# Scores of the wide layers cut into 64-row tiles, with the special keys in columns of their own

## What is computed

```python
q, k, v = x @ Wq, ctx @ Wk, ctx @ Wv              # (2048,1024), (1601,1024) twice; 16 heads of 64
logits = einsum('hqd,hkd->hqk', q, k) / 8
logits[:, :, token_indices_A] -= 20 * (1 - mask_A)[:, None]   # two keys
logits[:, :, token_indices_B] -= 20 * (1 - mask_B)[:, None]   # two keys
x = x + softmax(logits) @ v @ Wo + bo
```

## Time and profile before

| | us |
|---|---|
| median of 3 runs | 4620.56 |
| lowest, highest | 4617.27, 4621.11 |
| the profiled execution | 4619.93 |
| span of its trace | 4618.1 |

### The profile page before, as it was taken

One profiled execution on the slowest core, in us unless ns is written; L12 is line 12 of the kernel. 1 busy time (PEld: TensorE's weight loads), 2 busy tenths in 40 slices (PEclk: granted clock), 3 DMA queues, 4 the chain that ended last, 5 costly groups with the idle time before them and its releaser, 6 DMA issues.

```text
span 4618.1 us, 56243 instructions
## 1 busy us (share of the span) xinstructions
PE 4523.6 (98%) x20489; PEld 2807.1 (61%) x20489; DVE 2989.6 (65%) x5016; ACT 2262.0 (49%) x4016; POOL 2674.4 (58%) x1281
## 2 busy tenths in 40 slices
PE   8999999999999979999999999999999999999999
PEld 7888865555556545555556555555556655565554
DVE  3321467667766678778746667766767667676766
ACT  3222454454445436666655444444455545454443
POOL 0000367797778611111036887788774877788775
PEclk9999999999999979999999999999999999999999
DMA  4555832221222021011233221222216212222220
GB/s 151 178 188 163 289 79 64 66 68 45 66 64 52 12 39 16 12 15 16 58 109 111 67 67 45 64 68 52 52 46 221 63 39 64 64 68 54 58 48 28
DMA packets 124629, 349.64 MB, mean 76 GB/s; under 512 B 28085, under 2 KB 46005, under 8 KB 113338
## 3 DMA queue, kind: packets, MB, share of 16 engines
q1 hardware_dynamic: 124352, 346.04, 28.4%
HBM read 191.31 MB, written 120.31 MB: 67 GB/s over the span
## 4 chain that ended last, share of the span: by engine, by line
PE 95%; DVE 3%; DMA 1%; issue 1%; SPq 0%; ACT 0%; POOL 0%; DVEq 0%; ACTq 0%
PE ST L957 14%; PE SS L938 13%; PE ST L958 13%; PE OA L968 12%; PE OB L968 11%; PE ST L1090 5%; PE OA L1098 4%; PE SS L1003 4%; PE SS L1076 3%; PE OB L1076 1%; PE SS L977 1%; PE ST L1021 1%; PE ST L1022 1%; PE ST L1023 1%; DVE mpart L1599 1%; PE SS L925 1%
## 5 line engine op out<-in xcount | busy, mean ns | idle before, releaser
L838 POOL TENSOR_TENSOR acc<-acc,P 128x1024 f32<-128x1024 f32 x912 | 2203.2, 2448 | 598.4 <-DVE acc L1526 585.3
L1277 ACT ACTIVATE P<-ST 128x512 f32<-128x512 f32 (+1 forms) x2496 | 1465.4, 598 | 1305.4 <-PE ST L958 1169.8
L1499 DVE TENSOR_REDUCE mpart<-SS 128x1 f32<-128x400 f32 (+1 forms) x3072 | 1627.8, 569 | 676.2 <-PE SS L938 600.4
L938 PE MATMUL SS<-KS,QS 68*128 68x400 f32 (+1 forms) x3072 | 1037.9, 371 | 11.1 <-DMA QS<-stq 8.3
L957 PE MATMUL ST<-QX,KX 128*128 128x512 f32 (+1 forms) x2496 | 1032.9, 414 | 3.6 <-DMA QS<-mrow 2.0
L958 PE MATMUL ST<-QS,KS 69*128 69x512 f32 (+1 forms) x2496 | 989.0, 396 | 0.0
L938 PEld LDWEIGHTS SS<-KS,QS 68*128 68x128 f32 x3072 | 583.9, 190 | 222.6 <-DVE mpart L1499 33.5
L957 PEld LDWEIGHTS ST<-QX,KX 128*128 128x128 f32 (+1 forms) x2496 | 463.0, 185 | 389.2 <-issue 287.6
L968 PE MATMUL OA<-P,Vp 128*64 128x512 f32 (+1 forms) x2496 | 658.3, 606 | 0.0
L968 PE MATMUL OB<-P,Vp 128*64 128x512 f32 (+1 forms) x2496 | 641.3, 592 | 0.0
L1359 ACT ACTIVATE PG<-ST 128x512 f32<-128x512 f32 (+1 forms) x832 | 426.2, 616 | 213.3 <-PE ST L1090 213.0
(11 more groups left out here) (240 smaller groups left out, 4206.4 us busy)
## 6 DMA issues: line engine op xcount, KB each, us to landing
q_parts<-stq SPq DMA_DIRECT2D x96, 512.0 KB, 5.4
QX<-q_parts SPq DMA_DIRECT2D x96, 512.0 KB, 11.3
KX<-k_parts SPq DMA_DIRECT2D x48, 801.0 KB, 9.2
QS<-q_parts SPq DMA_DIRECT2D x45, 512.0 KB
R<-R SPq DMA_DIRECT2D x360, 64.0 KB, 2.0
v_tiles<-sv SPq DMA_DIRECT2D x24, 832.0 KB, 6.4
Vp<-v_tiles SPq DMA_DIRECT2D x24, 832.0 KB, 7.2
k_parts<-skh SPq DMA_DIRECT2D x48, 400.5 KB, 4.9
```

Source lines behind the costliest of these rows:

```text
L838: gp.tensor_tensor(out, out, P[0:k, slot(H, t), q, :], ALU.add).then_inc(pool_a, 1)
L938: pe.matmul(SS[at % 3][:, 0:w], QS[H % 3][0:SROWS, qt * 128:(qt + 1) * 128], KS[H % 3][0:SROWS, o:o + w], start=True, stop=True).then_inc( ...
L1277: act.activation(P[0:k, slot(H, t), j, :], ST[n % 3][0:k, :], ACT.Exp, scale=SCALE).then_inc(act_p, 1)
L1499: dve.tensor_reduce(mpart[H % 2][:, i // len(KCH), c:c + 1], SS[RING_AT["s", H, i] % 3][:, 0:w], AX.X, ALU.max).then_inc(dve_ss, 1)
```

## The change

**Row tiles.** Queries are split by column: columns 0 and 2 of 512 lie in partitions 0 to 63, columns 1 and 3 in partitions 64 to 127 (`QH` high parts, `QL` low parts). Keys (`KH` high, `KL` low) are loaded twice, into both halves. A unit becomes four matmuls of 64 rows (`score(H, t, j, i)`): KH x QH, KH x QL, KL x QH, and EXK x EXQ, which brings in maxima, penalty and a mask. A maxima tile becomes one matmul of 64 rows; only the last of a query tile's four has a second one, of 12 columns (`EXS`, `EXQ`).

**Order on TensorE.** `step_scores` writes the units in *half units*: pieces 0 and 1 of one unit alternate with pieces 2 and 3 of the unit before, the one in rows 0 to 63, the other in rows 64 to 127. Between two half units stands a maxima tile (fixed counts: 14, 14, 12, 12, 12 in the steps of head 0, then 4 and 10 in the last two steps of a head and 10 in each of five). Output tiles stand behind the values, each as two matmuls of 64 columns side by side; the transpose of the maxima stands ahead of its step's units.

**VectorE and GpSimd.** VectorE adds a third tile to the sums (tiles 1, 2, 3), GpSimd one less. In a step VectorE's additions for the sums come before those for the output, which are no longer between maxima. The reciprocals move one step later.

**Tokens.** Twelve columns for the special keys of the three wide layers are appended (1614 columns instead of 1602), the original ones are masked with -1e30. VectorE makes the tables for this at the start, and GpSimd gathers the context rows with 13 indirect DMAs in place of four plain loads by SyncE. The maxima's row is written with four DMAs instead of one, the penalty rows are no longer loaded for each head, and buffers lie elsewhere. In the first query phase ScalarE waits for earlier stores before it writes its fourth item.

The core of the diff:

```diff
-KP = NK + 1
-KCH = [(0, 402), (402, 400), (802, 400), (1202, 400)]
+NTOK = BIG * 4
+KX0 = NK + 1
+KP = KX0 + NTOK
+KCH = [(0, 402), (402, 400), (802, 400), (1202, 400 + NTOK)]
...
-    return [1, 2] if h + 1 < HEADS else [1, 2] + list(range(5, KT - 2))
+    return [1, 2, 3] if h + 1 < HEADS else [1, 2, 3] + list(range(6, KT - 2))
...
             def max_row(H):
                 sp.wait_ge(dve_ss, DVE_AT["m", H, 0])
-                sp.dma_start(words(QS[H % 3][MXROW:MXROW + 1, :]).rearrange("o (t p) -> o t p", p=128),
-                             words(mrow[:, :])).then_inc(d_m, 16)
+                for j in range(JQ):
+                    r, q = 64 * (j % 2) + MXROW, slice(j // 2 * 512, j // 2 * 512 + 512)
+                    sp.dma_start(words(EXQ[H % 2][r:r + 1, q]).rearrange("o (t p) -> o t p", p=128),
+                                 words(mrow[4 * j:4 * j + 4, :])).then_inc(d_m, 16)
...
+            for t in range(KT):
+                gp.indirect_dma_start(c_land[0:rows_of(t), t, :], None, a["ctx"][:, :],
+                                      bass.IndirectOffsetOnAxis(ap=t_row[0:rows_of(t), t:t + 1], axis=0))\
+                    .then_inc(d_cin[t], 16)
...
-                qt, (o, w) = i // len(KCH), KCH[i % len(KCH)]
-                pe.matmul(SS[at % 3][:, 0:w], QS[H % 3][0:SROWS, qt * 128:(qt + 1) * 128], KS[H % 3][0:SROWS, o:o + w],
-                          start=True, stop=True).then_inc(pe_s, 1)
+                r, q = slice(qt // 4 % 2 * 64, qt // 4 % 2 * 64 + 64), qt // 8 * 512 + qt % 4 * 128
+                o, w = KCH[c]
+                last = pe.matmul(SS[at % 3][:, 0:w], QH[H % 3][r, q:q + 128], KH[H % 3][r, o:o + w],
+                                 start=True, stop=o + w < KP)
+                if o + w == KP:
+                    last = pe.matmul(SS[at % 3][:, w - NTOK:w], EXQ[H % 2][r, q:q + 128], EXS[r, :], start=False, stop=True)
+                last.then_inc(pe_s, 1)
...
+            def score(H, t, j, i):
...
+                if i == 0:
+                    if t == 0 and j == 0:
+                        pe.wait_ge(d_x[H % 2], 64 * (H // 2 + 1))
...
+                    wait(pe, act_p, n - 2)
+                if i == 3 and t == 0 and j == 0:
+                    pe.wait_ge(d_m, 64 * (H + 1))
+                r, q = slice(j % 2 * 64, j % 2 * 64 + 64), slice(j // 2 * 512, j // 2 * 512 + 512)
+                left, right = ((KH[H % 3], QH[H % 3]), (KH[H % 3], QL[H % 2]), (KL[H % 2], QH[H % 3]), (EXK, EXQ[H % 2]))[i]
+                last = pe.matmul(ST[n % 3][0:k, :], left[r, t * 128:t * 128 + k], right[r, q], start=i == 0, stop=i == 3)
+                if i == 3:
+                    last.then_inc(pe_st, 1)
+
+            def step_scores(H, todo, HS, tiles):
...
+                middle, rounds = tiles[2:-2], len(todo) // 2 - 1
+                for u in range(0, len(todo), 2):
+                    mine = [middle[m] for p in part((len(tiles) - 4) // 2, u // 2 - 1, rounds) for m in (2 * p, 2 * p + 1)] \
+                        if tiles and u > 0 else []
+                    for i in range(2):
+                        score(H + todo[u][0], *todo[u][1:], i)
+                        if u > 0:
+                            score(H + todo[u - 1][0], *todo[u - 1][1:], 2 + i)
+                        elif tiles:
+                            s_tile(HS, tiles[i])
+                    for m in mine[:len(mine) // 2]:
+                        s_tile(HS, m)
+                    for i in range(2):
+                        if u > 0:
+                            score(H + todo[u + 1][0], *todo[u + 1][1:], i)
+                            score(H + todo[u][0], *todo[u][1:], 2 + i)
...
+                for i in range(2):
+                    if tiles:
+                        s_tile(HS, tiles[len(tiles) - 2 + i])
+                    score(H + todo[-1][0], *todo[-1][1:], 2 + i)
```

More of the change, by code:

```diff
@@ L87, in q_tiles, with o_items @@
     return part(SUNITS, q - S_FROM, S_TO - S_FROM) if S_FROM <= q < S_TO else range(0)
[L90 to L94, removed]
+def o_items(h, g):
+    return range(4 * g, 4 * g + 4) if h % 2 == 1 and h >= 3 and g < 2 else range(0)
 def takes_row(h, g, u):
@@ L145, in ring_order @@
             for g in range(STEPS):
[L146 to L152, removed]
+                if takes_row(h, g, 0):
+                    out.append(("m", first + h + 1, 0))
+                ahead, tiles = s_tiles(h, g)
+                out += [("s", first + h + ahead, i) for i in tiles]
+                out += [("o", l * PAIRS + (h - 3) // 2, i) for i in o_items(h, g)]
                 if takes_sums(h, g):
@@ L458, in s_loaded @@
         def s_loaded(H):
-            return sum(16 * (7 if i % HEADS == 0 else 4) for i in range(H % 3, H + 1, 3))
+            return sum(16 * (6 if i % HEADS == 0 else 4) for i in range(H % 3, H + 1, 3))
         def r_spread(H):
@@ L1002, in output @@
                 wait_ring(pe, at)
-                pe.matmul(SS[at % 3][:, :], wo[n % 2][:, ct * 128:(ct + 1) * 128], On[:, j * 512:(j + 1) * 512],
-                          start=True, stop=True).then_inc(pe_o, 1)
+                for c in range(0, 128, 64):
+                    last = pe.matmul(SS[at % 3][c:c + 64, :], wo[n % 2][:, ct * 128 + c:ct * 128 + c + 64],
+                                     On[:, j * 512:(j + 1) * 512], start=True, stop=True)
+                last.then_inc(pe_o, 1)
             def q_phase(l):
@@ L1037, in head @@
                 for g in range(STEPS):
-                    for u, (on, t, j) in enumerate(units(h, g)):
-                        scores(H + on, t, j)
-                        if takes_row(h, g, u):
-                            transpose_max(H + 1)
-                        if o_item(h, g, u) is not None:
-                            output(l * PAIRS + (h - 3) // 2, o_item(h, g, u))
-                        ahead, tiles = s_tiles(h, g, u)
-                        for i in tiles:
-                            s_tile(H + ahead, i)
+                    if takes_row(h, g, 0):
+                        transpose_max(H + 1)
+                    ahead, tiles = s_tiles(h, g)
+                    if units(h, g):
+                        step_scores(H, units(h, g), H + ahead, tiles)
                     pe.wait_ge(act_p, HU * H + JQ * (PV[g][-1] + 1))
@@ L1313, in q_phase @@
                     act.wait_ge(pe_q, n + 1)
+                    if l == 0 and q == 3:
+                        for b in range(2):
+                            act.wait_ge(d_wqo[b], 32 * (BIG * PAIRS // 2))
+                        act.wait_ge(d_k[0], k_stored(NW - 2))
+                        act.wait_ge(dve_k, 4 * (NW - 2))
                     if q >= NSTG:
```

387 lines of the change are left out of this document (268 added, 119 removed).

## The result

| | before | after |
|---|---|---|
| median of 4 runs, us | 4619.35 | 4985.08 |
| lowest, highest | 4617.27, 4621.11 | 4967.05, 4987.90 |
| span of the profiled execution | 4618.1 | 4983.5 |

The changed kernel takes 1.078 of the time before (95% interval 1.076 to 1.080). The forecast was 4751, the range 4500 to 4930. The direction was right, the size was not: +366 us and not +131.

A forecast was written before the change was run, and what follows sets the result against it. TensorE, busy 98% of the span, was taken as the bound: only its order and waits set the time. 4620 + 121 for three wide layers + 10 of small terms gave 4751 us; range 4500 to 4930.

The forecast's parts named there:

- rival 2: Matmuls in different row halves do not overlap: stream 9.56 us, about +380 a layer, some 5760 us; chance 8%.
- The chain of 0.43 + 0.60 + 0.15: Three score banks: last piece to ScalarE's start, its exponential, TensorE's restart; 1.18 us, two units every 1.415, stream 6.13.
- steps of four units: Short steps of a wide layer: 3.11 us against 2.87, 14 x 0.24 = +3.4 us a layer.
- rival 1: Score banks do not bind: half units at 0.56 us, stream 5.14, the change gains, 4440 us; chance 24%.
- cost nothing on the path: VectorE's third sums tile and GpSimd's one less: VectorE 44.3 + at most 4.64, GpSimd 52.9 - 2 x 2.45, both under 64.
- the risk for which the range had kept 20: VectorE's first additions end at 11.9, after the next step's first two maxima tiles: up to 0.5 us a head.
- The query phases: From first to last matmul of `xh` with `wqh` in each wide layer: forecast 0 us.
- Rival 3: Row halves overlap, but more waits than summed: VectorE's lateness, 12-column matmuls, query-phase mode changes; 4800 to 4930 us; chance 10%.
- fill the waits: Five first streams of head 0: their 12 to 14 maxima tiles lie in TensorE's waits, so 0 us added.
- the 12-column matmuls: 16 extra weight loads a head: fall into the waits, or up to 0.1 us each, 70 us, kept for the range.
- The term of the outputs: Output tiles behind the values cost 4 x 0.86 = 3.44 us; 9.57 against 9.68, -5.3 us a layer.
- the +3.7 at the start: Before the first key projection: token tables and 13 indirect DMAs, taken as +3 us, bounds -2 and +15.

The follow-up runs named there:

- Four banks: The changed kernel with four banks for scores and two for maxima, sums and outputs, instead of three and three: 4925.37 us, ratio 1.0669.
- both edits: The changed kernel with the reciprocals one step earlier and the additions cut as in the kernel before: 4819.65 us, ratio 1.0432.
- the best: The changed kernel with four score banks, two maxima banks, reciprocals one step earlier and additions cut as in the kernel before: 4719.82 us, ratio 1.0223.

## Why the prediction was right and wrong

**Right: overlap and chain.** Row halves overlap fully, so rival 2 falls. The Trainium skill, TensorE: Matmul & The Clock Gate, Part 3, has distinct row groups start about 4 ns apart; the trace agrees to the 0.01 us that it shows. The chain of 0.43 + 0.60 + 0.15 held: 1.42 to 1.43 between starts instead of 1.415, streams 6.20 instead of 6.13, 6.01 instead of 5.94, steps of four units 2.99, without the transpose of the maxima ahead of them, instead of 3.11. Four banks showed that it was the bound, so rival 1 falls with it. That agrees with the sentence in the Trainium skill, TensorEngine Tiling (Array Packing), Performance Considerations, that the prediction quoted.

**The step that failed** is what the sum put at nothing outside TensorE's own order. It says "VectorE's third tile and GpSimd's one less cost nothing on the path", from busy sums of 44.3 and 52.9 against more than 64, and before that "GpSimd's large sum of busy time is no bound: it works on sums that are needed a step and more later". The reciprocals, which the change moves one step later in VectorE's order, have no term at all, though the front of this document names the move. A busy sum can't show what they cost: the divisions start after the reciprocal plus 6.6 us of spreading, need three times 6.13 until the last one starts, and must end before ScalarE copies the next head's values. Before the change the reciprocal starts 20.9 us after the first values of head 36, and the last division ends at 3874.5, 6.1 us ahead of the copy of `OB`. A step is 9.8 us after the change, more than this room. Measured: the move costs 165 us with the additions cut as before, 96 with VectorE's third tile, and 206 in the kernel before. A part of that, by the estimate above at most 56 of the 165, is that TensorE's clock falls behind the long waits; the sum had no term for the clock either.

**"Costs nothing" was true of the third tile only in the changed kernel.** There it lies under the late divisions (4984 with and without). Without them it costs 69. Of these 43 are the stream behind the reciprocals, 7.22 instead of 6.20 in heads 1 to 14 of each layer, where VectorE's reductions come too late. That is the risk for which the range had kept 20. The rest lies in second streams of single heads, which are up to 4 us longer, and was not taken apart.

**Three terms mis-sized.** What is left when both are undone is 4820, 69 above the forecast of 4751:
- The query phases were put at 0 and cost 21 there (75.9, 63.2, 62.6), in the second and third 0.20 for each group of two tiles. Rival 3 named this; the sum did not hold it.
- The first steps of head 0 were put at 0, since their 12 to 14 maxima tiles would "fill the waits". There are more of them than the waits have room for: the streams are 7.5, 7.39 and three of 7.0 instead of 6.2 to 6.6, 3.7 a layer. VectorE's eleven reductions there run without a gap (5.43 us).
- A head's streams are 0.07 over the forecast, and 0.12 more in the two steps that have four of the 12-column matmuls and not two; the prediction had left these at nothing in the sum and up to 0.1 each in the range. The transpose, now ahead of the units, shows with 0.21, so that a step of four units takes 3.20 in all. Together with head 0 the heads are 1084 a layer instead of 1032 + 38.4 = 1070: 3 x 14, 42 us.

The term of the outputs held: values and outputs together take 7.02 with both edits, 3.44 more than values alone, forecast 3.44; but in the changed kernel the additions of VectorE were late behind its 4.9 us of sums, and the first such stretch of a head was 7.3 to 9.1 instead of 7.02. That too went with the two edits.

**Rival 3** was the nearest, more waits than summed, with 10% and 4800 to 4930; it named VectorE's lateness, never GpSimd's, and its range too ends below the 4985 measured.

Open: the +3.7 at the start, the 10 us or so around the group layer and the slow first query phase were not tried alone; that phase takes 80.4 from its first matmul to the first unit in the changed kernel, and anything from 75.9 to 88.0 in the versions above. No run separates the waits from the fall of the clock behind them. No version beat the kernel before; the best was 4720.

## What to carry to other kernels

For every moved instruction, follow what it feeds to the end, with its DMA issues, and compare the arrival with the moment it is needed; an engine at half load says nothing on that. When a tuned order is shortened on one engine, ask which buffer's release sets the pace next: here ScalarE's banks, then VectorE's reductions. A long wait of TensorE is paid twice when its clock falls behind it, so read the granted clock beside the waits. And undo lateness before judging a part: the third tile and the fourth bank looked cheap or weak as long as the divisions were late.

## What the chip showed that was not expected

- Going from full-width to 64-row matmuls and back costs: in the query phase 0.385 us for a pair of tiles (0.09 before it, 0.19 at it, 0.10 behind it).
- The clock of TensorE fell to 1.2 GHz at many of the waits at a head's start (0.50 at 4106.40 to 4113.20, around the wait of 2.25 us shown); before the change, and with both edits, it stayed at 2.4 GHz over all heads of the wide layers.
- The same two additions of VectorE take 2.35 us (4119.47, GpSimd idle, kernel with both edits) or 4.94:

```profile
4328.50 4.94 DVE L1743 TENSOR_TENSOR acc<-P 128x1024 f32<-128x1024 f32 x2
...
4322.02 10.33 POOL L951 TENSOR_TENSOR acc<-acc,P 128x1024 f32<-128x1024 f32 x4
```

  GpSimd's own additions, 2.35 each elsewhere, take 2.6 on average in that group, the last of its four 3.35. The two engines add at the same time there; what they share was not tried.
- Exponentials of 128 x 512 follow each other at 0.48 to 0.50 us, though each is listed with 0.60.
